# A graph network on one core: exponentials transposed and messages made at the head of the first phase's step

## The chip, the core and the metric

The kernel runs on one core of a Trainium2 chip. The core has five engines with queues of their own: TensorE (PE in the profile, its weight loads PEld), VectorE (DVE), ScalarE (ACT), GpSimd (POOL) and SyncE (SP), and 16 DMA engines. The metric is the device time of one execution in microseconds, lower is better. The runs before took 2203.87, 2203.7 and 2195.6 us; their median is 2203.7.

## The reference

Two graph layers with a residual and a normalisation over 128 channels behind each. There are 6250 nodes and 106250 edges, sorted by destination.

```
x = layernorm(x + L0(x, w1, w2, a, src, dst))
x = layernorm(x + L1(x, edges, edge_attr, edge_weight, ...))

L0: hi = x[src] @ w1;  hj = x[dst] @ w2              # 8 heads of 16 channels
    logits  = sum over a head of leaky_relu(hi + hj, 0.3) * a
    seg_max = segment_max(logits, dst)
    e       = exp(logits - seg_max[dst])
    attn    = e / segment_sum(e, dst)[dst]
    out     = segment_sum(hi * attn, dst)
L1: ef  = (relu(edge_attr @ We1 + be1) @ We2 + be2) * sigmoid(w * Wt + bt)
    msg = relu(concat(x[src], ef) @ Wn1 + bn1) @ Wn2 + bn2
    out = segment_sum(msg, dst) + x
```

The change touches only L0, the first phase.

## The kernel before

Every engine has its own program; they meet at semaphores. A prologue makes `hi = x @ w1` and writes it to `hi_rows` in memory, and keeps `x @ w2` in the tile `T`.

**The first phase** goes over the edges in 208 quads of 512 edges. Three quads are a group of 1536 edges, so there are 70 groups. GpSimd gathers the rows of `hi_rows` for a group with 12 indirect DMAs of 128 rows each (L707), into one of four slots of `G`. The gathers of group f wait until the messages of group f - 4 are made, because these read the same slot. GpSimd does nothing else in the phase.

The other engines run a software pipeline. In step g (`run_steps`, g from 0 to 68) they work on three groups at once: on the new group f = g, on group b = g - 1 and on group p = g - 2. The counter s = g mod 4 also gives each step one part of the node work of blocks that are complete:

- *New group f, one quad j at a time:* TensorE (`sums`, L1826 and L1831) transposes the four gathered tiles into the bank `U[j]` and adds `hj` by one-hot products. Inside or behind it stand products that bring a quad's logits into the bank `LT` (L1787). ScalarE (`scaled`, L895) writes 0.3 times the sums to `V`, VectorE (`leaky`, L1307) takes the larger of both. `nxt` (L1290) makes the block one-hots of the next group.
- *Group b:* VectorE runs four scans (L1348, L1365, L1369, L1376) that give every edge the maximum of its segment, with two small products on TensorE between them (L1900, L1909). Then it subtracts the maximum (`XM`, L1380), and ScalarE takes the exponential (`EXT`, L935) as the last thing of the step. VectorE's last work for the group is the window one-hots `oh` (L1389).
- *Group p:* TensorE transposes the exponentials into `EXp` (L1869), ScalarE copies them to `EXs` (L917), VectorE multiplies `EXp` by the gathered rows into `msg` (L1336), one product of 1536 columns. TensorE sums messages and exponentials by destination (`aggregate`, L1854 and L1858, three times a step), VectorE adds these sums to `acc` (L1318, L1320).
- *Node work:* s = 0 copies, transposes and divides three node blocks (behind the step's one-hots VectorE takes their moments, L1419 and L1424), s = 1 and its end normalise them (L1430), s = 2 and s = 3 turn them and multiply them by the next layer's weights; the rows `y_rows` are written.

Before the change a step's order at its head is, on TensorE: sums of quad 0, transpose of the exponentials, sums of quad 1. On ScalarE: `scaled(0)`, copy to `EXs`, `scaled(1)`. On VectorE: `leaky(0)`, `nxt(0)`, message product, `leaky(1)`, `nxt(1)`. TensorE's wait for `s_xm` ahead of its first sums protects the `LT` bank; it is for the maxima of group f - 2, which are subtracted in the step before.

Behind step 68 a part written out by hand finishes the last three groups and the last node blocks, writes the last `y_rows`, and then the second phase starts. There GpSimd gathers rows of `y_rows` in another 831 indirect DMAs (L741). Neither is touched.

Of the kernel before, what the change touches and what calls it, by code (L numbers as in the profile page):

```python
# [6 lines left out]
ACT = mybir.ActivationFunctionType  # L7
# [5 lines left out]
P = 128  # L13
# [23 lines left out]
BR = P  # L37
QR = 32 // HEADS
# [14 lines left out]
MB, MLAG = 3, 3  # L53
# [13 lines left out]
def need(eng, sem, value):  # L67

    if is_int(value) and value <= 0:
        return  # L70
    eng.wait_ge(sem, value)


def build(nc, x, src, dst, attr, ew, w1, w2, a, We1, be1, We2, be2, Wt, bt, Wn1, bn1, Wn2, bn2,
          hi_d, y_d, x1_d, rel_d, scan_d, max_d, sum_d, agg_d, out):
    with ExitStack() as ctx:
# [24 lines left out]
        EXT = sb("EXT", [P, P])  # L101
# [6 lines left out]
        ident = sb("ident", [P, P])  # L108
# [7 lines left out]
        AwP = sb("AwP", [P, 64 - HEADS])  # L116
# [65 lines left out]
        def chunk_buffers(at):  # L182
# [15 lines left out]
        accH = acc[:, 0, :]  # L198
# [62 lines left out]
        s_exp = sem("exponentials_ready")  # L261
        s_ext = sem("exponentials_transposed")
        s_exs = sem("exponentials_copied")
        s_oh = sem("window_onehots_ready")
        s_msg = sem("messages_ready")
# [33 lines left out]
        s_n = {"x": s_mx[0], "copy": s_m["nm"], "zero": s_m["cl"], "t": s_m["gT"], "max": s_m["dmax"], "rd": s_m["rd"],  # L299
               "att": s_m["gat"], "xs": s_m["xs"], "st": s_m["st"], "mv": s_m["mv"], "nr": s_m["sd"],  # L300
               "rs": s_m["rs"], "x1": s_m["x1"], "kept": s_mx[1], "xT": s_m["xT"], "xTc": s_m["xTc"],
               "y": s_m["y"], "ys": s_m["ys"], "stored": s_yw[0], "back": s_yw[1], "one": s_m["ve"]}
# [13 lines left out]
        def passed(eng, name):  # L316

            eng.sem_inc(s_passed[name], 1)
# [461 lines left out]
        def _(act):  # L780
# [99 lines left out]
            with act.Else():  # L880
                act.wait_ge(s_tab, 1)
                act.activation(acc[:, 0, NP // 2:NP], AwP[:, 0:1].to_broadcast([P, NP - NP // 2]), ACT.Copy
                               ).then_inc(s_zero, 1)

                def step(g, s, n, m):
                    f, b, p = stage(g, 0), stage(g, 1), stage(g, 2)
                    nq = quads(f) if f is not None else 0

                    def scaled(j):
                        if j >= nq:  # L890
                            return
                        act.wait_ge(s_u, f * GQ + j + 1)

                        need(act, s_log, (f - 1) * GQ + j + 1)
                        act.activation(V[:, j, :], U[j][:, :], ACT.Copy, scale=0.3).then_inc(s_v, 1)  # L895

                    nodes = m is not None and (not is_int(m) or m < MC)
                    if nodes and s == 0:

                        act.wait_ge(s_acc, 2 * GQ * (g - 3))  # L900
                        need(act, s_n["y"], m)
                        need(act, s_n["t"], m)
                        passed(act, "act")
                        cut = bass.ds(m * (MB * P), MB * P)
                        act.activation(mT[:, :], accH[:, cut], ACT.Copy)
                        act.activation(mD[:, :], accD[:, cut], ACT.Copy).then_inc(s_n["copy"], 1)
                    scaled(0)
                    if nodes and s == 1:
                        act.wait_ge(s_n["copy"], m + 1)
                        passed(act, "act")  # L910
                        act.activation(accH[:, bass.ds(m * (MB * P), MB * P)], AwP[:, 0:1].to_broadcast([P, MB * P]),
                                       ACT.Copy).then_inc(s_n["zero"], 1)
                    if p is not None:
                        act.wait_ge(s_ext, p + 1)

                        need(act, s_agg, GQ * p)
                        act.activation(EXs[:, :, 1:DC],  # L917
                                       EXp[:, HALO * HEADS:(HALO + GT) * HEADS].rearrange("p (t h) -> p t h", h=HEADS),
                                       ACT.Copy).then_inc(s_exs, 1)
                    scaled(1)  # L920
                    if nodes and s == 2:
                        act.wait_ge(s_n["xT"], m + 1)
                        act.activation(mT[:, :], AG[1][:, 0:MB * P], ACT.Copy).then_inc(s_n["xTc"], 1)
                    scaled(2)
                    if f is not None and (not is_int(f) or f + RG < NG):

                        stage_idx(f + RG, s)
                    if is_int(g) and g == NG - 2:
                        act.wait_ge(s_u, NQ)
                        act.wait_ge(s_log, NQ - GQ)  # L930
                        act.activation(V[:, 0, :], U[0][:, :], ACT.Copy, scale=0.3).then_inc(s_v, 1)
                    if b is not None:
                        act.wait_ge(s_xm, b + 1)
                        need(act, s_ext, b)
                        act.activation(EXT[0:BR, :], XM[0:BR, :], ACT.Exp).then_inc(s_exp, 1)  # L935
                run_steps(act, step)

                A, Z, O = NG - 3, NG - 2, NG - 1
                def kept(p, bank, to):
                    cnt = quads(p) * 4  # L940
                    act.wait_ge(s_ext, p + 1)
                    act.wait_ge(s_agg, GQ * min(p, Z))
                    act.activation(to, bank[:, HALO * HEADS:(HALO + cnt) * HEADS].rearrange("p (t h) -> p t h", h=HEADS),
                                   ACT.Copy).then_inc(s_exs, 1)

                def raised(b):
                    act.wait_ge(s_xm, b + 1)
                    act.wait_ge(s_ext, b)
                    act.activation(EXT[0:BR, :], XM[0:BR, :], ACT.Exp).then_inc(s_exp, 1)
                kept(A, EXp, EXs[:, :, 1:DC])  # L950
                act.wait_ge(s_n["copy"], MC)
                act.activation(accH[:, (MC - 1) * MB * P:MC * MB * P], AwP[:, 0:1].to_broadcast([P, MB * P]),
                               ACT.Copy).then_inc(s_n["zero"], 1)
                raised(Z)
                kept(Z, EXp, EXs[:, :, 1:DC])
                raised(O)
                act.wait_ge(s_n["one"], 1)
                kept(O, EXO, exsO[:, :, 1:DC])
                act.wait_ge(s_n["xT"], MC)
                act.activation(mT[:, :], U[1][:, 0:MB * P], ACT.Copy).then_inc(s_n["xTc"], 1)  # L960
                act.wait_ge(s_n["xT"], MC + 1)
                act.activation(V[:, 1, :], ps[7][:, :], ACT.Copy).then_inc(s_n["xTc"], 1)
# [53 lines left out]
        def _(dve):  # L1016
# [265 lines left out]
            with dve.Else():  # L1282
# [13 lines left out]
                def step(g, s, n, m):  # L1296
# [4 lines left out]
                    def leaky(j):  # L1301
                        if j >= nq:
                            return
                        dve.wait_ge(s_v, f * GQ + j + 1)

                        need(dve, s_log, (f - 1) * GQ + j + 1)
                        dve.tensor_tensor(E[:, j, :], U[j][:, :], V[:, j, :], ALU.max).then_inc(s_lk, 1)  # L1307
# [16 lines left out]
                    def nxt(j):  # L1324
                        if j < nxq:
                            block_onehot(nx, (s + 1) % RG, n + (s + 1) // RG, j)
                    leaky(0)
                    nxt(0)
                    if p is not None:

                        dve.wait_ge(s_exs, p + 1)

                        need(dve, s_agg, GQ * p)
                        cnt = quads(p) * 4
                        ex = EXp[:, HALO * HEADS:(HALO + cnt) * HEADS]
                        dve.tensor_tensor(msg[:, 0:cnt * C].rearrange("p (a c) -> p a c", c=HC),  # L1336
                                          ex.unsqueeze(2).to_broadcast([P, cnt * HEADS, HC]),
                                          G[:, (s - 2) % RG, 0:cnt * C].rearrange("p (a c) -> p a c", c=HC),
                                          ALU.mult).then_inc(s_msg, 1)
                    leaky(1)  # L1340
                    nxt(1)
                    if b is not None:
# [314 lines left out]
        def _(pe):  # L1657
# [125 lines left out]
            with pe.Else():  # L1783
# [17 lines left out]
                def step(g, s, n, m):  # L1801
# [40 lines left out]
                    def aggregate(j):  # L1842
# [16 lines left out]
                                            oh[:, t * W:(t + 1) * W], start=(i == 0), stop=(i == 3))  # L1859
                        ins.then_inc(s_agg, 1)  # L1860
                    bs, bn_ = (s - 1) % RG, n + (s - 1) // RG
                    if f is not None:

                        need(pe, s_xm, f - 1)
                    sums(0, b, bs, 2)
                    if p is not None:
                        pe.wait_ge(s_exp, p + 1)
                        need(pe, s_msg, p)
                        pe.transpose(EXp[:, 0:BR].rearrange("p (r k h) -> p k r h", r=QR, k=QR), EXT[0:BR, :], ident[0:BR, 0:BR]).then_inc(s_ext, 1)  # L1869
                    sums(1)  # L1870
                    nodes = m is not None and (not is_int(m) or m < MC)
                    if nodes and s != 1:
# [263 lines left out]
```

## Time and profile before

| | |
|---|---|
| median of the runs | 2203.7 us |
| profiled execution, its own time | 2198.74 us |
| its span | 2196.7 us |
| TensorE busy | 1779.1 us, 81% |
| VectorE busy | 1325.3 us, 60% |
| GpSimd busy | 1602.8 us, 73% |
| ScalarE busy | 659.2 us, 30% |

"Busy" counts instructions of an engine; for TensorE weight loads stand apart. The idle time of a row is that of the engine just ahead of these instructions, with what ended it. "issue" is waiting for nothing that the profile shows. The granted clock (PEclk) is a share of full speed.

### The profile page before, as it was taken

How to read it: one execution, taken by the hardware profiler on the slowest of the kernel's cores; microseconds unless marked ns; L12 is line 12 of the kernel's file. 1: busy time of each engine (PE TensorE's matmuls, PEld its weight loads, DVE VectorE, ACT ScalarE, POOL GpSimd, SP SyncE). 2: the span in 40 equal slices, each digit the busy share in tenths (PEclk: the TensorE clock that was granted, in tenths of full speed). 3: DMA queues.
4: the chain of work that ended last, by engine and by line, in shares of the span. 5: the costliest groups of instructions: out<-in, count | busy, mean ns of one | idle time of the engine just before them, and what ended most of it. 6: DMA issues, size and time to landing. Idle time of an engine off the chain costs nothing.

```text
span 2196.7 us, 47111 instructions
## 1 busy us (share of the span) xinstructions
PE 1779.1 (81%) x12650; PEld 1394.1 (63%) x12721; DVE 1325.3 (60%) x3725; ACT 659.2 (30%) x1410; POOL 1602.8 (73%) x1701
## 2 busy tenths in 40 slices
PE   6787777777888888877869888888888788888877
PEld 5465555655666666655657667666666676667666
DVE  6555666666556666656645456666566566665655
ACT  6111111121111111111114434434444344444432
POOL 5777777777777777777527777777777777777775
PEclk9889998999888888899879999989999999999998
DMA  8722333333333333333255444444444444454441
GB/s 238 153 78 85 84 95 84 96 97 91 89 94 86 96 97 87 91 90 96 56 142 154 139 126 139 129 135 135 141 127 131 137 132 137 128 142 127 141 125 46
DMA packets 239385, 252.30 MB, mean 115 GB/s; under 512 B 141011, under 2 KB 187720, under 8 KB 239315
## 3 DMA queue, kind: packets, MB, share of 16 engines
q1 hardware_dynamic: 185036, 141.15, 21.8%
q0 software_dynamic: 54000, 110.28, 19.4%
q8 instruction: 30, 0.49, 0.1%
q14 instruction: 31, 0.25, 0.0%
q10 hardware_dynamic: 288, 0.13, 0.0%
HBM read 233.20 MB, written 13.22 MB: 112 GB/s over the span
## 4 chain that ended last, share of the span: by engine, by line
POOL 54%; issue 23%; PE 11%; DVE 5%; DMA 4%; DVEq 1%; POOLq 1%; ACT 1%; SPq 0%; ACTq 0%
POOL T L741 32%; POOL G L707 21%; PE ps L1854 2%; DMA G<-hi_rows,idx 2%; PE ps L1831 2%; PE ps L1826 2%; PE ps L1858 1%; PE ps L1787 1%; DVEq L1316 1%; DVE msg L1336 1%; ACT V L895 0%; DMA T<-y_rows,idx 0%; PE ps L2060 0%; DMA out<-T 0%; PE ps L2069 0%
## 5 line engine op out<-in xcount | busy, mean ns | idle before, releaser
L741 POOL DMA_INDIRECT T<-y_rows,idx x831 | 788.1, 948 | 307.3 <-issue 251.8
L707 POOL DMA_INDIRECT G<-hi_rows,idx x831 | 799.7, 962 | 263.2 <-issue 249.5
L2060 PE MATMUL ps<-G 128*128 128x64 f32 x1664 | 223.0, 279 | 125.9 <-DVE acc L1613 125.0
L999 ACT ACTIVATE G<-G 128x512 f32<-128x512 f32 x208 | 131.1, 630 | 577.6 <-DVE G L1619 577.6
L2060 PEld LDWEIGHTS ps<-G 128*128 128x128 f32 x1664 | 211.9, 199 | 137.8 <-issue 137.2
L1826 PE MATMUL ps<-ident,G 128*128 128x128 f32 x828 | 147.9, 307 | 180.0 <-issue 92.8
L1619 DVE TENSOR_TENSOR G<-ps,T 128x512 f32<-128x512 f32 x208 | 143.6, 690 | 218.8 <-DMA T<-y_rows,idx 207.4
L2069 PE MATMUL ps<-wN,G 128*128 128x128 f32 x1664 | 254.2, 300 | 23.2 <-DVE T L1578 23.2
L895 ACT ACTIVATE V<-ps 128x512 f32<-128x512 f32 x207 | 123.7, 598 | 468.3 <-PE ps L1831 462.6
L1307 DVE TENSOR_TENSOR V<-ps,V 128x512 f32<-128x512 f32 x207 | 141.8, 685 | 184.5 <-ACT V L895 181.9
L2081 PEld LDWEIGHTS ps<-msg,wE 128*128 128x128 f32 x832 | 170.2, 205 | 127.2 <-issue 112.3
L1854 PEld LDWEIGHTS ps<-oh,msg 128*128 128x128 f32 x1608 | 230.8, 217 | 31.7 <-issue 23.7
L1854 PE MATMUL ps<-oh,msg 128*128 128x64 f32 x1608 | 244.6, 302 | 0.7 <-issue 0.3
L1826 PEld LDWEIGHTS ps<-ident,G 128*128 128x128 f32 x828 | 101.9, 155 | 220.2 <-issue 217.0
L2069 PEld LDWEIGHTS ps<-wN,G 128*128 128x128 f32 x1664 | 222.5, 208 | 25.4 <-DVE G L1629 25.0
L2075 PE MATMUL ps<-msg,wE 128*128 128x512 f32 x416 | 238.4, 658 | 0.0
L2081 PE MATMUL ps<-msg,wE 128*128 128x256 f32 x832 | 225.1, 395 | 0.0
L1831 PE MATMUL ps<-ohT,T 128*128 128x512 bf16 x552 | 175.5, 425 | 14.1 <-issue 13.8
L1318 DVE TENSOR_TENSOR acc<-ps,acc 128x64 f32 x201 | 45.2, 225 | 207.4 <-PE ps L1858 107.1
L994 ACT ACTIVATE G<-T,cols 128x512 f32<-128x512 f32 x208 | 166.8, 802 | 0.0
L1629 DVE SCALAR_TENSOR_TENSOR G<-ps,cols,G 128x512 f32<-128x512 f32 x208 | 154.9, 745 | 9.3 <-PE ps L2075 6.7
L1006 ACT ACTIVATE msg<-ps,cols 128x512 f32<-128x512 f32 x208 | 140.1, 673 | 38.5 <-PE ps L2081 38.1
(238 smaller groups left out, 2238.7 us busy)
## 6 DMA issues: line engine op xcount, KB each, us to landing
T<-in_edge_weight SPq DMA_DIRECT2D x103, 512.0 KB
Dbc<-block_destinations SPq DMA_DIRECT2D x69, 384.0 KB
T<-in_edge_attr SPq DMA_DIRECT2D x103, 256.0 KB
G<-hi_rows,idx POOLq DMA_INDIRECT x831
T<-y_rows,idx POOLq DMA_INDIRECT x831
link<-scan_destinations SPq DMA_DIRECT2D x280, 16.1 KB
hi_rows<-T SPq DMA_DIRECT2D x12, 256.0 KB, 4.6
mX<-in_x SPq DMA_DIRECT2D x15, 192.0 KB
```

The source lines that it names most:

```text
L707: pool.indirect_dma_start(out=G[:, s, t * C:(t + 1) * C], out_offset=None, in_=hi_d[:, :], in_offset=bass.IndirectOffsetOnAxis(ap=idx[:, s ...
L741: pool.indirect_dma_start(out=Yb[:, r, t * C:(t + 1) * C], out_offset=None, in_=y_d[:, :], in_offset=bass.IndirectOffsetOnAxis(ap=idx[:, r ...
L994: act.activation(twS[i], ewB[:, rr, :], ACT.Sigmoid, bias=cols[:, 4:5], scale=cols[:, 3:4]).then_inc(s_b["tw"], 1)
L1619: dve.tensor_tensor(zS[i], zP[i][:, :], Yb[:, rr, :], ALU.add).then_inc(s_b["zs"], 1)
L1629: dve.scalar_tensor_tensor(out=efS[i], in0=efP[i][:, :], scalar=cols[:, 2:3], in1=twS[i], op0=ALU.add, op1=ALU.mult).then_inc(s_b["efs"], 1)
L1826: pe.matmul(U[j][:, i * P:(i + 1) * P], G[:, s, t * C:(t + 1) * C], ident[:, :], is_transpose=True, start=(i == 0), stop=False, skip_group ...
L1831: ins = pe.matmul(U[j][:, :], flatT[:, bass.ds(col + part * C, C)], ohT[:, j, :], start=False, stop=(part == 2), skip_group_check=True)
L1854: pe.matmul(AG[j % 2][:, 0:W], msg[:, t * C:(t + 1) * C], oh[:, t * W:(t + 1) * W], start=(i == 0), stop=(i == 3))
L2060: ins = pe.matmul(sums_of(g4), hS[i][:, n * C:(n + 1) * C], ohB[i][:, n * W:(n + 1) * W], start=(n == 0), stop=(n == 3))
L2069: ins = pe.matmul(zP[i][:, n * C:(n + 1) * C], efS[i][:, n * P:(n + 1) * P], wN1[:, 1, :], start=True, stop=True)
L2075: pe.matmul(efP[i][:, :], wE2[:, :], r1S[i], start=True, stop=True).then_inc(s_b["ef"], 1)
L2081: ins = pe.matmul(out1[:, n], wE1[:, n, :], atS[i].rearrange("p (t e) -> p t e", t=2), start=True, stop=True)
```

## The change

The three engines do the same instructions in another order. TensorE transposes the exponentials of group p ahead of the new group's first sums, and ahead of the wait that stands before these. ScalarE copies them ahead of `scaled(0)`. VectorE makes the messages ahead of `leaky(0)` and `nxt(0)`. The programs of GpSimd and SyncE are the same, and so is the part behind the last step.

```diff
@@ ScalarE
+                    if p is not None:
+                        act.wait_ge(s_ext, p + 1)
+
+                        need(act, s_agg, GQ * p)
+                        act.activation(EXs[:, :, 1:DC],
+                                       EXp[:, HALO * HEADS:(HALO + GT) * HEADS].rearrange("p (t h) -> p t h", h=HEADS),
+                                       ACT.Copy).then_inc(s_exs, 1)
                     scaled(0)
...
-                    if p is not None:
-                        act.wait_ge(s_ext, p + 1)
...
                     scaled(1)
@@ VectorE
-                    leaky(0)
-                    nxt(0)
                     if p is not None:
 
                         dve.wait_ge(s_exs, p + 1)
...
                                           ALU.mult).then_inc(s_msg, 1)
+                    leaky(0)
+                    nxt(0)
                     leaky(1)
                     nxt(1)
@@ TensorE
-                    if f is not None:
-
-                        need(pe, s_xm, f - 1)
-                    sums(0, b, bs, 2)
                     if p is not None:
                         pe.wait_ge(s_exp, p + 1)
                         need(pe, s_msg, p)
                         pe.transpose(EXp[:, 0:BR].rearrange("p (r k h) -> p k r h", r=QR, k=QR), EXT[0:BR, :], ident[0:BR, 0:BR]).then_inc(s_ext, 1)
+                    if f is not None:
+
+                        need(pe, s_xm, f - 1)
+                    sums(0, b, bs, 2)
                     sums(1)
```

## Rows read from the trace of the kernel before

**Rows 1.** The page: busy time of the engines, and the chain that ended last, by engine.

```profile
PE 1779.1 (81%) x12650; PEld 1394.1 (63%) x12721; DVE 1325.3 (60%) x3725; ACT 659.2 (30%) x1410; POOL 1602.8 (73%) x1701
...
POOL 54%; issue 23%; PE 11%; DVE 5%; DMA 4%; DVEq 1%; POOLq 1%; ACT 1%; SPq 0%; ACTq 0%
```

**Rows 2.** Busy time by stretch: stretch, length, busy us (instructions), granted clock, DMA share, GB/s.

```profile
31.50:1084.10 1052.60, 834.27 (x7103) 629.95 (x7172) 651.52 (x1690) 203.00 (x492) 799.70 (x831) 0.90 0.36 95
1084.10:1138.30 54.20, 42.19 (x269) 34.09 (x269) 27.75 (x96) 6.31 (x20) 0.01 (x1) 0.75 0.27 74
1138.30:2196.70 1058.40, 880.26 (x5106) 708.82 (x5106) 627.04 (x1885) 431.61 (x870) 788.07 (x831) 0.92 0.46 132
```

**Rows 3.** Line 707: ns minimum/median/maximum; then busy us, mean ns, idle before.

```profile
L707 POOL DMA_INDIRECT G<-hi_rows,idx x831: 940/945/1796, 31.5 to 1083.2; - x167
...
L707 POOL DMA_INDIRECT G<-hi_rows,idx x831 | 799.7, 962 | 263.2 <-issue 249.5 <-DMA hi_rows<-T 10.3 <-DVE msg L1336 3.4
```

**Rows 4.** Waits of POOL to 1139 us: total us, times, the longest.

```profile
POOL G L707 <- issue: 249.5, 819, 0.3
POOL T L741 <- DMA y_rows<-V: 54.2, 1, 54.2
...
POOL G L707 <- DVE msg L1336: 3.4, 11, 0.3
```

**Rows 5.** Waits of TensorE, 31 to 1084 us, same columns.

```profile
PE ps L1826 <- issue: 92.8, 68, 12.7
PE ps L1826 <- DMA G<-hi_rows,idx: 36.0, 13, 4.7
```

**Rows 6.** Timeline of one step (s = 3): start, duration, engine, line, operation [idle before].

```profile
1060.84 0.31 ACT L935 ACTIVATE EXT<-XM 128x128 f32<-128x128 f32 x1 [4.89 <-DVE XM L1380]
1061.51 0.65 PE L1826 MATMUL ps<-ident,G 128*128 128x128 f32 x4 [0.73 <-DVE XM L1380]
...
1063.33 0.27 PE L1869 MATMUL ps<-ident,EXT 128*128 128x128 f32 x1
...
1064.02 0.24 ACT L917 ACTIVATE EXs<-ps 128x96 f32<-128x96 f32 x1
1064.16 0.69 DVE L1307 TENSOR_TENSOR V<-ps,V 128x512 f32<-128x512 f32 x1 [1.40 <-issue]
...
1065.13 1.74 DVE L1336 TENSOR_TENSOR msg<-ps,G 128x1536 f32<-128x1536 f32 x1
...
1068.34 0.65 PE L1826 MATMUL ps<-ident,G 128*128 128x128 f32 x4 [2.44 <-DMA G<-hi_rows,idx]
```

**Rows 7.** Timeline of the step before it (s = 2): normalisation, first maximum, first logits.

```profile
1051.63 1.03 DVE L1430 TENSOR_SCALAR mX<-mX,mv,rs 128x128 f32<-128x128 f32 x3
1052.40 0.68 DVE L1307 TENSOR_TENSOR V<-ps,V 128x512 f32<-128x512 f32 x1
...
1053.25 0.36 PEld L1787 LDWEIGHTS ps<-V,AwP 128*32 128x32 f32 x10 [0.17 <-DVE V L1307]
```

**Rows 8.** Timeline of a step with s = 1: last moments and first maximum.

```profile
1033.54 0.32 DVE L1424 BATCH_NORM_AGGREGATE mv<-st 128x2 f32<-128x6 f32 x3 [0.15 <-DVE st L1419]
...
1034.18 0.69 DVE L1307 TENSOR_TENSOR V<-ps,V 128x512 f32<-128x512 f32 x1 [0.32 <-ACT V L895]
```

**Rows 9.** Timeline of the last full step: its third sums.

```profile
1082.60 0.65 PE L1826 MATMUL ps<-ident,G 128*128 128x128 f32 x4 [1.97 <-DMA G<-hi_rows,idx]
```

**Rows 10.** Timeline: a gather with the window one-hots, and a gather under a message.

```profile
1031.83 1.80 POOL L707 DMA_INDIRECT G<-hi_rows,idx  x1 [0.31 <-issue]
1031.86 0.94 DVE L1389 TENSOR_TENSOR oh<-iotaF,R 128x768 f32<-128x768 f32 x1
...
1066.64 0.94 POOL L707 DMA_INDIRECT G<-hi_rows,idx  x1 [0.30 <-issue]
```

**Rows 11.** Busy time by stretch in the tail, columns as in Rows 2.

```profile
1083.50:1098.50 15.00, 14.78 (x94) 12.11 (x94) 5.80 (x15) 2.17 (x5) 0.61 (x1) 0.54 0.05 9
1098.50:1114.50 16.00, 12.80 (x109) 10.53 (x107) 11.33 (x36) 1.07 (x4) 0.00 (x0) 1.00 0.06 17
```

More of the change, by code:

```diff
@@ L912, in step @@
                                        ACT.Copy).then_inc(s_n["zero"], 1)
-                    if p is not None:
-                        act.wait_ge(s_ext, p + 1)
[L916 to L919, printed above, removed]
                     scaled(1)
```

## The prediction

> **What bounds the kernel now.** I read the page first. It shows POOL at 73% busy and TensorE at 81% [rows 1], so the busy shares alone don't name the bound. The chain that ended last does: 54% of it is POOL, with the gathers at L741 (second phase) and L707 (first), and 23% "issue", which is mostly the fixed time between two of them. The table by stretches then cuts the span in four: 31.5 us before the first gather, 1052.6 us of first-phase gathers, 54.2 us in which POOL does nothing, and 1058.4 us of second-phase gathers [rows 2]. 31.5 + 1052.6 + 54.2 + 1058.4 = 2196.7 us, the span.
>
> In the first phase POOL issues 831 gathers, of median 945 ns and mean 962 ns [rows 3]. Between them lie 249.5 us in 819 gaps of 0.3 us, and the releaser "DVE msg" also stands only at gaps of 0.3 us (11 of them, 3.4 us), so no gather ever waited for a message [rows 4]. 799.7 us busy and 263.2 us of gaps, less the 10.3 ahead of the first [rows 3], are 1052.6 us: POOL is saturated from the first gather to the last. The first phase gets shorter only if a gather gets shorter or if the 54.2 us behind the last one do. The last wait in this stretch is POOL's, for `y_rows` [rows 4].
>
> TensorE is not the bound there. It stood 36.0 us in front of its first sums for gathered rows and 92.8 us for what the profile calls issue [rows 5], 128.8 us over 69 steps, or 1.9 us a step.
>
> **What the change does, part by part.** Nothing is added or taken away: each of the 67 steps has the same TensorE transpose of the exponentials, the same ScalarE copy, the same VectorE message product. Only their place in three queues changes. POOL and SyncE have the same program.
>
> *TensorE, the head of a step.* The transpose now stands ahead of the first sums and waits for this step's exponentials. In the step at 1060 us the exponentials start at 1060.84 and last 0.31, to 1061.15; the first sums started at 1061.51; the transpose of 0.27 came at 1063.33 [rows 6]. In the new order the transpose starts 0.2 to 0.5 after 1061.15 and lasts 0.27, so the first sums start at 1061.6 to 1061.9. That is 0.1 to 0.4 us later; I take 0.4, because the read of the table column stands behind the transpose. The second sums lose the transpose in front of them and get nearly all of it back. Behind the waiting transpose is the whole queue of TensorE, so everything up to the first logits moves by those 0.4 us.
>
> *ScalarE.* The copy to EXs (0.24 us) came behind the first scaling, at 1064.02 [rows 6]; it now comes at about 1062 and takes nothing from the first scaling, which waits for sums that end later. Cost 0; in a step with node work two copies stand ahead of it, but these end before VectorE is free.
>
> *VectorE, the message.* It lasts 1.74 us (1.75 below) and ran behind the first maximum and the first one-hot. Now it runs behind the previous step's last operation. Where VectorE idles there, it fits: in the step at 1060 us the message started at 1065.13, 0.97 after the first maximum at 1064.16 [rows 6]; moved up it fills the wait for sums, the first maximum goes 0.4 us later (with the sums) and the second about 1 us earlier. Where VectorE is busy with node work it doesn't fit. In the step at 1047 us the normalisation (1.03) starts at 1051.63 and the first maximum stands at 1052.40 [rows 7]. With the message between them, 1052.40 + 1.75 = 1054.15: the first maximum is 1.75 us late, the logits behind it (1053.25) are as late, and so are the third sums and the aggregates queued behind them. In the step at 1031 us the moments end at 1033.54 + 0.32 = 1033.86 and the maximum started at 1034.18 [rows 8]; the message would end at 1035.61, so 1.4 us late. The fourth kind of step (node copy) has the maxima bound by VectorE later on; it gives back about as much as its head costs: 0 to 0.4.
>
> Sum over four steps: 0.4 + 1.75 + 1.4 + 0.4 = about 4 us, 1.0 us a step; the most it can be is 0.4 + 1.75 in each, 2.15. Against 1.9 us a step of waiting on TensorE [rows 5] the 1.0 is hidden by the gathers, and even the extreme is nearly so. If that cover were gone, 1.0 x 67 = 67 us would show. The change makes the step longer, not shorter, and POOL hides it.
>
> *The gain it could bring on POOL.* Messages free the G buffers one to three us earlier. No gather waited for one, so this is worth 0.
>
> *The 54.2 us.* What counts is when the third sums of the last full step start. Before, this is 1082.60 after 1.97 us of waiting for gathered rows, and the same sums of the step before waited 2.44 us, to 1068.34 [rows 6, 9]. New: the step at 1047 us ends 1.75 later; the next one adds 0.4; 2.44 - 2.15 = 0.3 us of cover is left, so those sums still start at 1068.34. The last step adds 0.4 again: 1.97 - 0.4 = 1.6 us left, and its third sums start at 1082.60 as before. Behind them the order is not touched. Cost 0, bounds: 0, and about +2 us if the cover at 1068 fails by as much.
>
> *Gathers held up by VectorE.* The mean gather is 17 ns over the median, 831 x 0.017 = 14.4 us in all [rows 3]. The long ones lie under the window one-hots: the gather at 1031.83 took 1.80 us, and the one-hot from 1031.86 lasted 0.94, to 1032.80; the gather ended 0.83 after that. The message doesn't do this: the gather at 1066.64, under the message of 1065.13 to 1066.87, took the usual 0.94 [rows 6, 10]. The change moves when one-hots fall against gathers in the steps that don't wait for rows. A one-hot of 0.95 with a random place in the pitch of 1.25 would hold a gather by (0.84 x 0.84 / 2) / 1.25 = 0.28 us on average (it holds one that starts inside it, up to 0.12 before its end), an estimate from these rows; 68 of them make 19 us, and some 7 more from scans and one-hots in bf16, estimated the same way. So the 14.4 us can become anything from nearly 0 to 26. I keep 14.4, as steps that wait for gathered rows keep their rhythm; ends: -14 and +12 us.
>
> The Trainium skill (SBUF — State Buffer, "Who interferes with whom") says that a VectorE operation with two SBUF inputs holds up only a GpSimd instruction that reads SBUF, since the second input takes just the read side of a shared port pair; it infers that generating descriptors needs the write side and is therefore left alone. By that inference the one-hot would hold no gather, and this term would be 0 in both kernels and at both ends. This trace disagrees, with 1.80 against 0.94 us.
>
> Sum: 0 (gathers) + 0 (last step) + 0 (tail). On the profiled run's own 2198.74 us (span 2196.7 and 2.0 around it) that gives 2198.7. The runs shown have their median 5.0 us above this and spread over 8.3 us; I forecast against the median: 2203.
>
> **The rivals.** Under 0.5% (11 us) a measurement of this kernel can't tell from no change.
>
> *The one-hots fall worse* (slower). Place: POOL's gathers in the first phase. If their placement becomes random, the 14.4 us become 26: 2203.7 + 12 = 2216. It decides from a mean gather of about 975 ns on (831 x 0.013 = 11 us). For it: the long gathers in [rows 10] are real, and the present figure is under the random one. Against: the rhythm of most steps is set by the rows' landing, and the order from there to the one-hot is the same. Chance 0.07.
>
> *The step becomes the bound* (slower). If TensorE falls to its lower clock in more steps, each longer by some us, the 0.9 us a step of cover left is gone; with 0.5 us over, 67 x 0.5 = 34 us: 2237. For it: the granted clock in the first phase is 0.90, so such stretches exist [rows 2]. Against: they are in the 1.9 us already. Chance 0.04.
>
> *The tail gets another clock* (faster, or a little slower). From 1083.5 to 1098.5 the granted clock was 0.54, near the 1.2 GHz level, with TensorE busy for 14.78 us, after it had waited 1.97 us for rows; in the next 16 us it was 1.00 [rows 9, 11]. If this stretch ran at 2.4 GHz, at most half of 14.78 would go: -7 us, 2196; if the next fell instead, up to +6. Both stay inside 0.5%. With good luck on the one-hots (-7 or more) it would be 2189 or less: chance 0.07.
>
> *The change does nothing for the message*, since it must wait for the exponentials anyway. Then all stays as it is, 2203, and this can't be told apart by the time, only by the trace.
>
> **How the numbers follow.** Forecast (hidden by POOL, whatever the tail's clock does) 0.82, one-hots worse 0.07, step the bound 0.04, both lucky 0.07. Range: the forecast's own is 2196 - 2 to 2203 + 8; to leave only 2 in 10 out I take 2192 to 2215. Faster by over 0.5% 0.08, within 0.5% 0.81, slower 0.11.
>
> **What would show it.** Right: the message starts some 2 us after the maxima are subtracted, the first maximum of the steps with normalisation 1.75 us later, the gap between gathers still 0.3 us, TensorE's waits for gathered rows smaller by some 1 us a step, POOL's idle stretch 50 to 58 us. Wrong: a gap of more than 0.3 us ahead of a gather in the first phase, a mean gather over 975 or under 950 ns, or third sums in the last full step that start without waiting for rows.

## The result, and the profile after

The changed kernel takes 2204.9 us (median of 10 runs, 2202.47 to 2212.19); the kernel before, on the same chip, 2199.17 us (10 runs, 2194.6 to 2203.87). The ratio is 1.0029, with a 95% interval of 1.0018 to 1.0040: 5.7 us more. That is under the 0.5% that the prediction set as its bound, but ten runs on each side resolve it. The change made the kernel slightly slower; the forecast was no change. The forecast's number, 2203, stood on three runs of the kernel before with a median of 2203.7; with ten runs that median is 2199.17.

The page of the changed kernel: busy time, chain, and the row of the first phase's gathers.

```profile
PE 1809.9 (82%) x12720; PEld 1396.3 (63%) x12721; DVE 1334.6 (61%) x3725; ACT 664.3 (30%) x1410; POOL 1611.0 (73%) x1701
...
POOL 54%; issue 22%; PE 11%; DVE 6%; DMA 3%; DVEq 2%; POOLq 1%; ACT 1%; SPq 0%; ACTq 0%
...
L707 POOL DMA_INDIRECT G<-hi_rows,idx x831 | 808.0, 972 | 263.5 <-issue 251.7
```

POOL's share of the chain is the same 54% as in [rows 1]. Its 831 gathers now take 808.0 us instead of 799.7, mean 972 ns instead of 962 [rows 3]; the time between them, 263.5 us, did not move. Next, the stretches of the changed kernel: first phase's gathers, POOL's idle stretch, second phase (columns as in [rows 2]).

```profile
30.80:1091.80 1061.00, 868.25 (x7172) 632.88 (x7172) 658.49 (x1690) 207.90 (x491) 808.02 (x831) 0.88 0.35 95
1091.80:1142.60 50.80, 38.44 (x274) 31.14 (x272) 27.76 (x96) 6.47 (x20) 0.02 (x1) 0.84 0.29 80
1142.60:2201.70 1059.10, 880.77 (x5106) 710.93 (x5106) 629.29 (x1885) 431.71 (x870) 787.93 (x831) 0.92 0.46 132
```

Against [rows 2], stretch by stretch, in us:

| | before | after | difference |
|---|---|---|---|
| ahead of the first gather | 31.5 | 30.8 | -0.7 |
| first phase's gathers | 1052.6 | 1061.0 | +8.4 |
| POOL idle | 54.2 | 50.8 | -3.4 |
| second phase | 1058.4 | 1059.1 | +0.7 |
| span | 2196.7 | 2201.7 | +5.0 |

The gathers of the first phase cost 8.4 us, all of it their own duration (8.3 us), and the idle stretch gave 3.4 back. POOL's waits in the changed kernel (total us, times, the longest) confirm that no gather waited for a message there either:

```profile
POOL G L707 <- issue: 251.7, 826, 0.3
POOL T L741 <- DMA y_rows<-V: 50.8, 1, 50.8
...
POOL G L707 <- DVE msg L1334: 1.2, 4, 0.3
```

What makes a gather long is seen in the timeline of the changed kernel, with a window one-hot and a message:

```profile
165.17 0.96 DVE L1389 TENSOR_TENSOR oh<-iotaF,R 128x768 f32<-128x768 f32 x1
165.36 1.58 POOL L707 DMA_INDIRECT G<-hi_rows,idx  x1 [0.30 <-issue]
166.04 1.75 DVE L1334 TENSOR_TENSOR msg<-ps,G 128x1536 f32<-128x1536 f32 x1
167.25 0.94 POOL L707 DMA_INDIRECT G<-hi_rows,idx  x1 [0.30 <-issue]
```

The kernel's tiles lie in two memories, SBUF and PSUM; those that a row calls `ps` are in PSUM. The gather at 165.36 begins under the one-hot, which reads two tiles in SBUF (`iotaF` and `R`), and takes 1.58 us. It ends at 166.94, 0.81 after the one-hot's end at 166.13, as the gather of [rows 10] did. The gather at 167.25 begins under the message, which reads one operand from PSUM, and takes 0.94. Going through both timelines and counting the gathers that begin between 0.12 us ahead of a one-hot and 0.12 us ahead of its end gives 31 before, which cost 9.0 us over their normal duration (15 of them took over 1.25 us), and 45 after, which cost 17.4 us (30 over 1.25). The 8.4 us between the two costs are the 8.3 us of the table.

By kind of step the cost went from 3.4 to 4.2 us (s = 0), from 2.8 to 4.7 (s = 1), from 0 to 3.2 (s = 2) and from 2.8 to 5.4 (s = 3). In the old order none of the 17 one-hots of the s = 2 steps held a gather; 13 of them started 0.31 to 0.32 us after a gather did, so that the next one began when they were almost over. In the new order 8 of the 17 held one.

The longer step is there too, and hidden. In the changed kernel's step with normalisation (s = 2):

```profile
1059.26 1.03 DVE L1430 TENSOR_SCALAR mX<-mX,mv,rs 128x128 f32<-128x128 f32 x3
1060.04 1.75 DVE L1334 TENSOR_TENSOR msg<-ps,G 128x1536 f32<-128x1536 f32 x1
1061.70 0.68 DVE L1307 TENSOR_TENSOR V<-ps,V 128x512 f32<-128x512 f32 x1
```

From the normalisation to the first maximum it is 2.44 us; it was 0.77 in [rows 7]. TensorE's waits from 31 to 1091 us and its third sums in the last full step show a part of what absorbed it:

```profile
PE ps L1826 <- issue: 78.9, 89, 12.9
...
PE ps L1787 <- DVE V L1307: 31.0, 36, 1.7
PE ps L1826 <- DMA G<-hi_rows,idx: 25.8, 11, 3.0
```

```profile
1090.42 1.11 PE L1826 MATMUL ps<-ident,G 128*128 128x128 f32 x4 [1.84 <-DMA G<-hi_rows,idx]
```

The two kinds of waiting ahead of L1826 that the prediction added up to 128.8 us [rows 5] are now 104.7. That is 0.36 us a step less, not the 1.0 that the prediction named as a sign of being right; 31.0 us are now spent in front of the logits for a maximum (4.6 before). The last step's third sums still wait 1.84 us for rows (1.97 in [rows 9]).

### The profile page after: what moved, and what is told of

Its sections match the earlier page's. It is cut to its first block, busy times and chain, and to the rows that moved or that the text cites. A ratio compares the mean times of both kernels' runs of the same rounds, so it can differ in the third digit from the quotient of the medians.

```text
span 2201.7 us, 47210 instructions
## 1 busy us (share of the span) xinstructions
PE 1809.9 (82%) x12720; PEld 1396.3 (63%) x12721; DVE 1334.6 (61%) x3725; ACT 664.3 (30%) x1410; POOL 1611.0 (73%) x1701
## 4 chain that ended last, share of the span: by engine, by line
POOL 54%; issue 22%; PE 11%; DVE 6%; DMA 3%; DVEq 2%; POOLq 1%; ACT 1%; SPq 0%; ACTq 0%
POOL T L741 29%; POOL G L707 26%; PE ps L1854 2%; PE ps L1831 1%; PE ps L1826 1%; DMA G<-hi_rows,idx 1%; DMA T<-y_rows,idx 1%; PE ps L2069 1%; PE ps L1858 1%; PE ps L1787 1%; DVEq L1316 1%; PE ps L2081 1%; PE ps L2060 1%; PE ps L2075 1%; DVE msg L1334 1%
## 5 line engine op out<-in xcount | busy, mean ns | idle before, releaser
L707 POOL DMA_INDIRECT G<-hi_rows,idx x831 | 808.0, 972 | 263.5 <-issue 251.7
L1826 PE MATMUL ps<-ident,G 128*128 128x128 f32 x828 | 156.2, 320 | 115.5 <-issue 78.9
L1854 PEld LDWEIGHTS ps<-oh,msg 128*128 128x128 f32 x1608 | 220.7, 208 | 27.1 <-issue 18.1
L1854 PE MATMUL ps<-oh,msg 128*128 128x64 f32 x1608 | 232.9, 292 | 0.0
L1826 PEld LDWEIGHTS ps<-ident,G 128*128 128x128 f32 x828 | 111.6, 163 | 168.2 <-issue 160.4
L1831 PE MATMUL ps<-ohT,T 128*128 128x512 bf16 x621 | 199.1, 437 | 0.0
L1787 PE MATMUL ps<-V,AwP 128*32 128x128 f32 x1940 | 135.9, 315 | 31.4 <-DVE V L1307 31.0
```

The costliest lines, as they stand in the source:

```text
L707: pool.indirect_dma_start(out=G[:, s, t * C:(t + 1) * C], out_offset=None, in_=hi_d[:, :], in_offset=bass.IndirectOffsetOnAxis(ap=idx[:, s ...
L1787: return pe.matmul(LT[at % 2][k:k + 32, 0:P], AwP[:, 32 - (r + 1) * HEADS:64 - (r + 1) * HEADS], E[:, j, i * P:(i + 1) * P], start=start, ...
L1826: pe.matmul(U[j][:, i * P:(i + 1) * P], G[:, s, t * C:(t + 1) * C], ident[:, :], is_transpose=True, start=(i == 0), stop=False, skip_group ...
L1831: ins = pe.matmul(U[j][:, :], flatT[:, bass.ds(col + part * C, C)], ohT[:, j, :], start=False, stop=(part == 2), skip_group_check=True)
L1854: pe.matmul(AG[j % 2][:, 0:W], msg[:, t * C:(t + 1) * C], oh[:, t * W:(t + 1) * W], start=(i == 0), stop=(i == 3))
```

## The experiments

The theory after the result: the first phase is as long as its gathers, and a gather that begins under a VectorE operation with two SBUF operands is held until that operation is over. The new order places the one-hots differently against the gathers, and more of them collide. The rivals: the longer step reaches POOL in places (a wait); the loss is in the tail's clock; or the message at the head, whatever it does to the one-hots, costs the 5.7 us.

**Take the second SBUF operand away, in both orders.** The ramp `iotaF` is copied once into an unused part of a PSUM bank and the one-hots read it there. The arithmetic is the same. `e1_before_iota_psum` has this in the old order, `e2_after_iota_psum` in the new one.

```diff
+        iotaP = AG[0][:, 448:448 + W]
...
+                dve.wait_ge(s_hic, NU + 1)
+                dve.tensor_copy(iotaP, iotaF[:, :]).then_inc(s_lc, 1)
+                dve.wait_ge(s_lc, 1)
...
-                                          iotaF[:, :].unsqueeze(1).to_broadcast([P, cnt, W]),
+                                          iotaP.unsqueeze(1).to_broadcast([P, cnt, W]),
```

> The kernel before, but the window one-hots read the row of numbers (iotaF) from PSUM, in columns of the first aggregate bank that nothing else uses, so that they have one SBUF input instead of two. Theory 1 (a one-hot with two SBUF inputs holds every gather that starts inside it): the 8.9 us that gathers lose under the one-hots vanish, the 4 to 5 us under the scans stay. Mean gather 962 -> about 951 ns, first gather to last 1052.6 -> about 1044 us, time about 2199 - 9 = 2190 us. Theory 2 (the longer step is what costs in the changed kernel, and long gathers have another cause): mean gather stays at 962 ns and the time at 2199 us, or a little over, since VectorE reads PSUM.

> The changed kernel with the same edit. Theory 1: the 17.4 us under the one-hots vanish, mean gather 972 -> about 950 ns, time about 2205 - 17 = 2188 us; the two orders come within 3 us of each other. Theory 2: the changed order stays 5 to 6 us slower than the old one with the same edit, about 2205 us.

Measured: old order 2186.54 us (7 runs), ratio to before 0.9944 [0.9924, 0.9965]; new order 2187.2 us (8 runs), 0.9946 [0.9927, 0.9964]. The 5.7 us between the orders are gone (the means of the two differ by 0.1 us, give or take an estimated 3.4 from their scatter), and both are 12 us under the kernel before, the fastest versions of this study. The page's gather rows, old order and then new:

```profile
L707 POOL DMA_INDIRECT G<-hi_rows,idx x831 | 792.9, 954 | 263.3 <-issue 248.3 <-DMA hi_rows<-T 10.4 <-DVE msg L1340 4.6
```

```profile
L707 POOL DMA_INDIRECT G<-hi_rows,idx x831 | 791.0, 952 | 263.3 <-issue 249.6 <-DMA hi_rows<-T 10.3 <-DVE msg L1338 3.4
```

and the timeline of the new order with the PSUM operand, where a gather begins inside a one-hot:

```profile
93.19 0.94 DVE L1393 TENSOR_TENSOR oh<-ps,R 128x768 f32<-128x768 f32 x1
...
93.99 0.94 POOL L707 DMA_INDIRECT G<-hi_rows,idx  x1 [0.31 <-issue]
```

In these two runs 41 and 38 gathers begin under a one-hot by the same count, and none takes more than 0.95 us. The one-hot itself costs what it did (0.94 to 0.96). The step of the new order is as long as in the change, and it costs nothing here. So the collision with the one-hots is the cause, and the message at the head as such is not. One remainder: the profiled gather stretch of the old order fell by 6.8 us (1052.6 to 1045.8) while the medians fell by 12.3; its profiled execution took 2192.49 us, the slowest of its seven, so the stretches of one execution are good to a few us only. And of the 9.0 us that the one-hots gave up, 2.2 went to gathers held by other operations, so that 6.8 are left.

Some long gathers are left. In the same kernel the last scan of the step (L1380) reads `link` and `R`, both in SBUF:

```profile
1005.89 0.47 DVE L1380 TENSOR_TENSOR_SCAN R<-link,ps,R 128x128 f32<-128x128 f32 x1
1005.95 1.17 POOL L707 DMA_INDIRECT G<-hi_rows,idx  x1 [0.30 <-issue]
```

Gathers that begin under this scan cost 3.9 us before the change, 3.7 after it, 4.9 and 3.5 with the ramp in PSUM, and 4.1 and 1.5 in the next two kernels: small, and not what differs.

**Move TensorE and ScalarE alone.** `e3_te_act_only` has the transpose and the copy at the head, VectorE as before.

```diff
@@ ScalarE
+                    if p is not None:
+                        act.wait_ge(s_ext, p + 1)
...
                     scaled(0)
@@ TensorE
+                    if p is not None:
+                        pe.wait_ge(s_exp, p + 1)
...
                     sums(0, b, bs, 2)
```

> Only TensorE's transpose and ScalarE's copy move to the head of the step; VectorE makes the messages behind the first maximum and the first one-hot as before. The step gets about 0.4 us longer instead of 1.0. Theory 1: the time follows the placing of the one-hots, which this alone should change little: mean gather 960 to 967 ns, 2198 to 2203 us. Theory 2: 0.4 of the 1.0 us a step, so about 40% of the 5.7 us: 2201 us. What tells them apart is whether the time follows the sum of the gathers' extra.

Measured: 2200.23 us (12 runs), ratio 1.0006 [0.9992, 1.0019]: no difference in time. The gather row says more:

```profile
L707 POOL DMA_INDIRECT G<-hi_rows,idx x831 | 806.1, 970 | 263.3 <-issue 244.1 <-DMA hi_rows<-T 10.4 <-DVE msg L1336 8.8
```

The mean gather was 970 ns, nearly the changed kernel's, where I had expected 960 to 967: a miss. Here 39 gathers begin under one-hots and cost 15.0 us. The time stayed because POOL's idle stretch was 49.2 us instead of 54.2. So this smaller edit, which lengthens the step by some tenths of a us only, already shifts the placement. The collisions depend on how one-hots and gathers fall against each other, and how much an edit changes that could not be told from what the edit does. The time alone decides nothing here: the rival expected 2201 us.

**Move VectorE alone.** `e4_dve_only` makes the message ahead of the first maximum, while the transpose and the copy keep their old places behind the first sums.

```diff
@@ VectorE
-                    leaky(0)
-                    nxt(0)
                     if p is not None:
...
+                    leaky(0)
+                    nxt(0)
```

> Only VectorE's message moves ahead of the first maximum; TensorE's transpose stays behind the first sums and ScalarE's copy behind the first scaling. The message must then wait for EXs (1064.26 in the step at 1060 us) and the first maximum for the message: 1064.3 + 1.75 = 1066.05 instead of 1064.16, 1.9 us late in every kind of step. Four steps without waits for rows lasted some 53.6 us (12.4 + 14.0 + 12.4 + 14.8), against 60.8 for their gathers; with 4 x 1.85 they come to 61. If POOL is the bound with the cover I reckoned, the time stays within 2195 to 2215 and moves with the gathers' extra; if the step's length counts at once (theory 2), the 7.4 us in four steps show at the rate of the change's 4 us for 5.7: +10 us, 2210.

Measured: 2220.49 us (6 runs, 2212.7 to 2243.24), ratio 1.0104 [1.0061, 1.0147]. Its page row and POOL's wait:

```profile
L707 POOL DMA_INDIRECT G<-hi_rows,idx x831 | 805.3, 969 | 299.8 <-issue 244.7 <-DVE msg L1334 44.8 <-DMA hi_rows<-T 10.3
```

```profile
POOL G L707 <- DVE msg L1334: 44.8, 27, 4.8
```

```profile
720.11 1.75 DVE L1334 TENSOR_TENSOR msg<-ps,G 128x1536 f32<-128x1536 f32 x1
...
722.64 0.94 POOL L707 DMA_INDIRECT G<-hi_rows,idx  x1 [4.77 <-DVE msg L1334]
```

The timeline is that of its worst wait. This is what the prediction's second rival (the step becomes the bound) describes, reached by another way than TensorE's clock, which is 0.898 here and 0.900 in the change. The first maximum waits for a message that waits for exponentials turned behind the first sums, so the step gets longer than the gathers that hide it. 27 of POOL's gaps end with a message, 15 of them longer than the usual 0.3 us, 4.8 us at most. In the profiled execution (2241.95 us, one of the two slowest of the six) that is 36.5 us of idle time ahead of gathers (299.8 against 263.3) where the change has none. I had expected 2195 to 2215 us by one reckoning and 2210 by the other: a miss. From the subtraction of the maxima to the first maximum the mean rose by 8.2 us over the four kinds of step, where 7.4 had been reckoned. The moves belong together: without the transpose at the head, the message at the head breaks the cover.

**A second look at the orders and the operands, and one thing that stayed in the way.** Fourteen more runs were made in four later groups, each group on another chip than the first experiments: both orders again unchanged, both with the ramp and the scans' second operand in PSUM, and the order of `e3_te_act_only`.

```diff
+                        R2P = LT[bs % 2][:, P:2 * P]
...
-                        dve.tensor_tensor_scan(R2[0:BR, :], link[:, bs, 0:P], logit, shp[0:BR, 0:1], ALU.add,
+                        dve.tensor_tensor_scan(R2P[0:BR, :], link[:, bs, 0:P], logit, shp[0:BR, 0:1], ALU.add,
...
-                        dve.tensor_tensor_scan(R4[0:BR, ::-1], link[:, bs, P:0:-1], R2[0:BR, ::-1], shp[0:BR, 1:2],
+                        dve.tensor_tensor_scan(R4[0:BR, ::-1], link[:, bs, P:0:-1], R2P[0:BR, ::-1], shp[0:BR, 1:2],
```

In all four groups the kernel before itself took 3246 to 3352 us instead of 2199, so these runs can't test what happens at 2199 us; they show the same programs with another bound. The page of the unchanged kernel before in the first of these groups:

```profile
PE 2025.1 (61%) x12650; PEld 1524.4 (46%) x12721; DVE 1328.1 (40%) x3725; ACT 662.0 (20%) x1410; POOL 1588.6 (48%) x1701
...
another core or an unknown queue 31%; PE 30%; issue 15%; DVE 13%; DVEq 6%; SPq 1%; ACT 1%; DMA 1%; ACTq 0%
...
L707 POOL DMA_INDIRECT G<-hi_rows,idx x831 | 786.2, 946 | 1002.8 <-DVE msg L1336 694.4
```

```profile
POOL G L707 <- DVE msg L1336: 694.4, 60, 45.9
```

VectorE, ScalarE and POOL are busy for about as long as at 2199 us; POOL has left the chain; its gathers wait 694 us for messages, and hardly one is held (mean 946 ns): in none of the fourteen profiles does a gather begin under a window one-hot. Here the step is the bound of the first phase, and each edit is priced by what it does to the step. What was expected of each, and then the results in one table:

> The kernel before once more, unchanged, for a second profile of it. If the placing of its one-hots is a rhythm of the kernel and not luck of one execution, they hold gathers by about 9 us in all again (mean gather 960 to 964 ns) and the stretch behind the last gather is again 53 to 55 us. If it is luck, the figure can be anything from 9 to the 19 us of a random placing. Time 2199 us, ratio 1.000.

> The changed kernel once more, unchanged, in the same hour as the others. Rhythm: the one-hots hold gathers by about 17 us again (mean gather 970 to 974 ns), the stretch behind the last gather is again about 51 us. Luck: 9 to 19 us. Ratio 1.002 to 1.004, 2203 to 2206 us.

> The kernel before with the row of numbers in PSUM and with the second scan's result in PSUM too (free columns of the logits' bank), so that the third and fourth scans have one SBUF input instead of two. Theory 1: the some 5.5 us that gathers lose under these two scans also go, mean gather 954 -> about 948 ns, as in the second phase; time 2187 - 5 = 2182 us. Against it: if only long operations matter, it stays at 2187 us.

> The changed kernel with both edits. Theory 1: mean gather about 948 ns, time 2187 - 4 = 2183 us, and no difference beyond 3 us to the old order with both edits, since nothing is left that the order of VectorE's work can do to a gather. If the new order has a worth of its own behind the last gather (its tail was 2 to 3 us shorter in two profiles), it comes out 2 to 3 us under the old order here.

> The kernel before, unchanged, once more: the last job ran where the step, not POOL, was the bound (3348 us), and so said nothing of gathers held by one-hots. Where POOL is the bound again (about 2199 us): if the placing of the one-hots is a rhythm of this order, they hold gathers by about 9 us in all (mean gather 960 to 964 ns), and the stretch behind the last gather is 53 to 55 us; if it is luck of one execution, anything from 9 to 19 us.

> The changed kernel, unchanged, once more. POOL the bound: rhythm says 17 us under the one-hots again (mean gather 970 to 974 ns), luck says 9 to 19 us; ratio 1.002 to 1.004. The step the bound, as in the last job: ratio 1.007 again, 20 to 25 us slower, since then the message ahead of the first maximum shows.

> The old order with the row of numbers and the second scan's result in PSUM. POOL the bound, theory 1: mean gather 954 -> about 948 ns, time 2187 - 5 = 2182 us, ratio about 0.992. If only long operations hold gathers: 2187 us.

> The new order with both edits. Theory 1: mean gather about 948 ns, time 2183 us, within 3 us of the old order with both. A worth of the new order behind the last gather would show as 2 to 3 us under the old order here; a cost of its longer step, if it counted at all where POOL is the bound, as 2 to 6 us over it.

> TensorE's and ScalarE's move without VectorE's, again. POOL the bound (2199 us): 2198 to 2203 us, mean gather 960 to 970 ns. The step the bound (3350 us): if VectorE's message ahead of the first maximum is what costs there, this kernel costs only its 0.4 us a step of the 1.0, +6 to +10 us of the 20; if TensorE's wait for the exponentials is what costs, it costs the whole 20 us.

> The changed kernel again. POOL the bound: 2203 to 2206 us, mean gather 970 to 974 ns and 15 to 19 us under the one-hots if that is a rhythm, 9 to 19 if it is luck. The step the bound: +18 to +25 us.

> The old order with the row of numbers and the second scan's result in PSUM. POOL the bound: mean gather about 948 ns, 2182 us. The step the bound: no gain, 0 to -5 us, since POOL then waits for messages and a shorter gather frees nothing.

> The new order with both. POOL the bound: 2183 us, within 3 us of the old order with both. The step the bound: +18 to +25 us, like the changed kernel.

> The changed kernel, unchanged. POOL the bound (before at about 2199 us): 2203 to 2206 us, mean gather 970 to 974 ns with 15 to 19 us under the one-hots if their placing is a rhythm, 9 to 19 if it is luck. The step the bound (before at about 3250 or 3350 us): 20 to 60 us slower than before.

> The old order with the row of numbers and the second scan's result in PSUM. POOL the bound: mean gather about 948 ns, 2182 us, 5 us under the row of numbers alone. The step the bound: within 5 us of before.

| run | edit | us | ratio to before |
|---|---|---|---|
| `e5_before_again` | none | 3346.2 | 0.9994 [0.9963, 1.0025] |
| `e6_after_again` | the change | 3369.4 | 1.0074 [1.0052, 1.0095] |
| `e7_before_iota_scan_psum` | old order, PSUM operands | 3342.2 | 0.9977 [0.9948, 1.0006] |
| `e8_after_iota_scan_psum` | new order, PSUM operands | 3368.8 | 1.0055 [1.0032, 1.0079] |
| `e9_before_third` | none | 3354.7 | 1.002 [0.9988, 1.0053] |
| `e10_after_third` | the change | 3370.7 | 1.0066 [1.004, 1.0093] |
| `e11_before_iota_scan` | old order, PSUM operands | 3349.2 | 0.9996 [0.9968, 1.0024] |
| `e12_after_iota_scan` | new order, PSUM operands | 3372.1 | 1.0064 [1.0042, 1.0086] |
| `e13_te_act_again` | TensorE and ScalarE only | 3251.4 | 1.0012 [0.9985, 1.0039] |
| `e14_after_fourth` | the change | 3309.8 | 1.0193 [1.0146, 1.0241] |
| `e15_before_iota_scan` | old order, PSUM operands | 3253.5 | 1.0003 [0.9975, 1.003] |
| `e16_after_iota_scan` | new order, PSUM operands | 3309.1 | 1.0179 [1.0135, 1.0224] |
| `e17_after_fifth` | the change | 3370.7 | 1.0117 [1.0062, 1.0172] |
| `e18_before_iota_scan` | old order, PSUM operands | 3336.9 | 1.0007 [0.9975, 1.0039] |

Three things follow. Where the step is the bound, the new order is 0.6 to 1.9% slower in each of the four groups (18 to 64 us). TensorE's and ScalarE's part of it costs nothing that can be measured (1.0012, at most 13 us by its interval), so most of the 64 us that the change costs in that group come with VectorE's message ahead of the first maximum. And the PSUM operands gain nothing there (0.998 to 1.001 in the old order), as they must if they act only through gathers. Two expectations missed: `e14_after_fourth` and `e16_after_iota_scan` lost 64 and 63 us instead of 18 to 25; why that group differs is not known.

These runs do show one thing of the gathers. With the scans' second operand in SBUF, 48 of the 134 gathers that begin under the third and fourth scan take over 1.0 us (seven kernels, up to 1.13). With it in PSUM it is 1 of 161 (seven kernels), and that one begins as the scan ends, under the block one-hot behind it.

The waits of the change in such a run:

```profile
POOL G L707 <- DVE msg L1334: 731.8, 60, 45.2
```

The same 60 waits. Over the three groups with the kernel before at 3333 to 3352 us the five profiles with the new order have 728 to 732 us of them and the five with the old order 694 to 718, 709 on average: 21 us more, like the 18 to 22 us in the times of the first two groups, and 21 / 67 = 0.3 us a step. In the group at 3246 us it is 684 and 687 against 646: 39 us, 0.6 a step.

## Why the prediction was right and wrong

- *POOL bounds the phase and no gather waits for a message:* right before and after; the wait rows show it. The number was lucky: 2203 and the measured 2204.9 lie close because the forecast started from a median that was 4.5 us too high. Between the profiled executions, 2198.74 and 2203.4 us, the forecast of no change is off by 4.7.
- *The step gets 1.0 us longer:* right in sum, by the means, and nearly in its terms. From the subtraction of the maxima to the next first maximum the mean rose by 1.7 us in the steps with normalisation (predicted 1.75), 1.1 with moments (1.4), 0.8 with s = 3 (0.4) and 0.4 with node copies (0 to 0.4): 4.0 us over four steps against 4. Single steps scatter by more than that, and the medians would give 5.6. The shortest four steps in a row take 54.9 us, still under the 60.8 of their 48 gathers. `e2_after_iota_psum` shows that this costs no time while it is hidden, `e4_dve_only` what comes when it isn't.
- *The last full step and its third sums:* right; 1.84 us of waiting for rows, 1.6 predicted.
- *The tail:* taken at 0; it gave 3.4 us back (54.2 to 50.8) with the same instructions, and its rival was right in kind. The stretch that matches the first row of [rows 11] is 1091.20:1106.20; its clock is 0.91 instead of 0.54:

```profile
1086.00:1096.00 10.00, 8.16 (x61) 5.97 (x59) 5.02 (x14) 1.67 (x3) 4.55 (x5) 0.83 0.18 41
1091.20:1106.20 15.00, 13.80 (x125) 11.10 (x123) 8.23 (x18) 2.17 (x5) 0.57 (x1) 0.91 0.11 27
1096.00:1104.00 8.00, 6.80 (x69) 5.38 (x68) 5.78 (x13) 1.57 (x4) 0.00 (x0) 1.00 0.11 31
```

  The third maximum of the last full step starts 0.5 us after the last gather's end before and 1.7 after it in the change; from there to the end of POOL's idle stretch it is 53.8 and 49.1 us. In the four kernels of the first experiments, whose clock stayed at 1.00 for at least 14 us behind the last gather, that second part is 48.5 to 49.8 us. So the low clock ahead of 1098.5 us cost the profiled execution of the kernel before some 4 to 5 us. That is one profile of each kernel, and whether the order has a part in it is not shown.
- *Gathers held up by VectorE: "I keep 14.4, as steps that wait for gathered rows keep their rhythm":* this is the step that failed. The term was 799.7 - 831 x 0.945 = 14.4 us (the prediction's 831 x 0.017 is 14.1) and is 808.0 - 831 x 0.945 = 22.7 us now; it rose by 8.3. The mechanism was named and priced (up to +12, the rival *the one-hots fall worse*), and its threshold was set at a mean gather of 975 ns; the gather came to 972. What was wrong is to have taken the placement of the old order as given: 9.0 us under the window one-hots became 17.4. The reason given held for one kind of step only, s = 2, where no one-hot held a gather, and there it broke: 3.2 of the 8.4 us come from it. The old placement was better than random, for which the prediction's formula gives 19 us; and 31 gathers began in the counted places where random placing makes it 52 (68 x 0.96 / 1.25). The other three orders with two SBUF operands lie nearer to random: 45 gathers and 17.4 us in the change, 39 and 15.0 in `e3_te_act_only`, 44 and 16.7 in `e4_dve_only`. A step whose head moves by 0.4 to 1.7 us, against a pitch of 1.25, can't be expected to keep its phase; from a figure below the random one, up was the likelier way. Taking the random placing as the forecast (+12, less what the tail gives) would have named the direction, at about twice the size.

The Trainium skill (SBUF — State Buffer, "Who interferes with whom") infers that a tensor_tensor with two SBUF inputs leaves descriptor generation alone, as it takes only the read side. The runs disagree: the gather at 165.36 took 1.58 us under the one-hot with two SBUF inputs, and with one of them in PSUM the same one-hot held none of 79 gathers, and the kernel was 12 us faster. The general rule of the same section, that such an operation contends with a GpSimd instruction which reads SBUF, fits these runs.

What stays open. Whether 31 collisions before and 45 after are a property of each order or of one execution: there is one profile each at 2200 us. The ten-run medians (5.7 us apart) and their equality once the collision is removed speak for the order. The scans' second operand in PSUM frees the gathers, as the later runs show, but what that is worth in time (3 to 5 us by the count) was never measured with POOL as the bound. The 12.3 us that the old order gained in `e1_before_iota_psum` are more than the 9.0 counted under its one-hots; what gave the rest wasn't found. And why the kernel before took 3246 to 3352 us in the later groups, with nearly the same busy time on VectorE, ScalarE and POOL and idle time that the profile puts on "another core or an unknown queue", was not found.

## What to carry to other kernels

When GpSimd's gathers bound a phase, compare their mean with their median first, and list the VectorE operations with two SBUF operands that run beside them: moving one operand to PSUM gave 12 us here and takes the collision away, which a reordering only places anew. A step lengthened under the cover of such a bound is free until the cover is used up and then costs in full, so a change of order that gains nothing at the bound is a risk with nothing to win. And if a held-up time is below its random figure, expect an edit that moves the phase to raise it: here three other orders had 15.0 to 17.4 us where the old one had 9.0 and random placing makes it 19.

## What was not expected of the hardware

- A gather that begins while VectorE runs an operation with two SBUF operands ends about 0.82 us after that operation (0.83 in [rows 10], 0.81 at 165.36), against 0.94 for a whole gather: it seems to lose all but the first 0.12 us or so. With one operand in PSUM it loses nothing (0.95 at most, 79 gathers), and the operation is no slower.
- Now and then the one-hot loses instead. In eight places of four profiles (before, the change, `e3_te_act_only`, `e4_dve_only`) the gather begins within 0.04 us of the one-hot's start and takes the usual 0.94 to 0.95 us, while the one-hot takes 1.00 to 1.03 instead of 0.96. With the ramp in PSUM no one-hot takes over 0.96.
- Two SBUF operands are not the whole list: gathers that begin under the block one-hots (L1290), which read one bf16 tile, took up to 1.08 us and lost 1.3 us in all before the change.
- The same program on one core can take 2199 or some 3300 us. In the second case instructions last about as long on VectorE, ScalarE and POOL (1328.1, 662.0 and 1588.6 us busy), while the mean granted clock of TensorE is 0.76 instead of 0.90, a gather waits up to 45.9 us for one message, and engines stand for many us in front of work that nothing in the profile holds up.
